# A top-32 attention kernel: the doubt test of each score tile moves from VectorE to GpSimd, and ranked values are kept for three tiles

## The reference

```python
scores = jnp.einsum('bhqd,bhkd->bhqk', q, kk) * scale
vals, idx = jax.lax.top_k(scores, k)          # k = 32 of 3136
w = jax.nn.softmax(vals, axis=-1)
vg = jnp.take_along_axis(v[:, :, None, :, :], idx[..., None], axis=3)
out = jnp.einsum('bhqk,bhqkd->bhqd', w, vg)
```

## Time and profile before

| | us |
|---|---|
| median of 3 runs | 34495.23 |
| the profiled execution | 34476.98 |
| its span in the trace | 34475.4 |
| VectorE busy | 28043.8 |
| TensorE matmuls busy | 26639.3 |
| ScalarE busy | 23766.6 |
| GpSimd busy | 19614.1 |

### The profile page before, as it was taken

The page is one execution under the profiler, slowest core; times in us unless marked ns, Lnnn a source line. Parts: engine busy times, 40 slices in busy tenths (PEclk is TensorE's granted clock), DMA queues, the critical chain, the costliest instruction groups (busy, mean ns, idle before and its releaser), DMA issues. The chain is left out here.

```text
span 34475.4 us, 624959 instructions
## 1 busy us (share of the span) xinstructions
PE 26639.3 (77%) x190808; PEld 11994.5 (35%) x190809; DVE 28043.8 (81%) x155761; ACT 23766.6 (69%) x29153; POOL 19614.1 (57%) x7792
## 2 busy tenths in 40 slices
PE   4656887788888888887258887888887788872589
PEld 4543333333333333333123333333333333331122
DVE  5557999899999999997769998999998999986421
ACT  1116887788888889886158897988887788871111
POOL 0005776677777777775037776777776677760000
PEclk7778998899999999998579998999998899985555
DMA  1001000000000000000110000000000000001100
GB/s 40 8 21 45 6 6 5 5 6 6 6 6 5 6 6 6 6 5 25 43 54 6 6 6 5 6 6 5 5 5 5 5 6 6 6 13 50 52 11 8
DMA packets 133222, 455.07 MB, mean 13 GB/s; under 512 B 29244, under 2 KB 85444, under 8 KB 111240
## 3 DMA queue, kind: packets, MB, share of 16 engines
q1 hardware_dynamic: 129256, 410.72, 3.6%
HBM read 244.71 MB, written 165.93 MB: 12 GB/s over the span
## 5 line engine op out<-in xcount | busy, mean ns | idle before, releaser
L232 POOL TENSOR_SCALAR Z<-S,M 128x3136 uint8<-128x3136 f32 (+1 forms) x2240 | 18383.3, 8212 | 6122.5 <-PE banks L336 5801.1
L510 DVE MAX8 C<-S 128x8 f32<-128x98 f32 x102400 | 19731.9, 252 | 1892.4 <-ACT S L421 1747.0
L421 ACT COPY S<-banks 128x896 f32<-128x896 f32 (+1 forms) x12800 | 10277.1, 821 | 1898.6 <-DVE C L510 676.8
L451 ACT ACTIVATE W<-banks 128x1024 f32<-128x1024 f32 (+1 forms) x9524 | 9801.9, 1030 | 1718.1 <-PE banks L336 1652.1
L327 PE MATMUL banks<-Q,K 99*128 99x512 bf16 (+2 forms) x22550 | 6434.5, 370 | 2666.4 <-ACT S L421 1410.1
L289 PE MATMUL banks<-K,Q 96*128 96x448 bf16 x22400 | 6566.7, 371 | 1422.6 <-ACT W L451 554.8
L372 PE MATMUL banks<-W,V 128*32 128x512 f32 (+1 forms) x45100 | 6843.3, 587 | 109.0 <-ACT W L454 78.9
L336 PE MATMUL banks<-NEG,Z 128*128 128x128 bf16 (+1 forms) x56300 | 6022.8, 224 | 0.0
L336 PEld LDWEIGHTS banks<-NEG,Z 128*128 128x128 fp8e4 x56300 | 4587.2, 101 | 1761.4 <-issue 255.9
L336 PE MATMUL banks<-NEG,ZA 128*128 128x128 bf16 (+1 forms) x24150 | 4779.2, 223 | 0.0
L327 PEld LDWEIGHTS banks<-Q,K 99*128 99x128 bf16 (+1 forms) x22550 | 1639.0, 99 | 7460.5 <-ACT S L421 3616.4
(11 more groups left out here) (204 smaller groups left out, 20819.6 us busy)
## 6 DMA issues: line engine op xcount, KB each, us to landing
q<-ln_o SPq DMA_DIRECT2D x20, 1568.0 KB, 5.1
ln_x<-y SPq DMA_DIRECT2D x16, 1568.0 KB, 6.0
K<-k_parts SPq DMA_DIRECT2D x130, 147.0 KB
Q<-q_parts SPq DMA_DIRECT2D x130, 147.0 KB
q_parts<-pj_parts SPq DMA_DIRECT2D x24, 784.0 KB, 4.7
k_parts<-pj_parts SPq DMA_DIRECT2D x24, 784.0 KB, 7.8
V<-v_rows SPq DMA_DIRECT2D x130, 112.5 KB, 7.4
v_rows<-pj_vt SPq DMA_DIRECT2D x8, 1800.0 KB, 11.8
```

The lines of the kernel that those rows point to most:

```text
L232: pool.tensor_scalar(mask_at(tile)[0:rows, :].bitcast(U8), m.S[0:rows, slot(tile), :], m.M8[0:rows, side(i), t, 31:32], None, ALU.is_lt).t ...
L421: act.copy(m.S[0:rows, slot(tile), at:at + CW * w].rearrange("p (a n) -> p a n", a=w), m.AB[0:rows, pair(score_at[a]):pair(score_at[a]) + ...
L451: ins = act.activation(m.W[:, e % 4, 0:n_banks, :], m.AB[:, b:b + n_banks, :], ACT.Exp)
L510: ins = dve.max(m.C[0:rows, tile % 2, TOP_AT + k:RANKED:CHUNKS], m.S[0:rows, slot(tile), CHUNK * k:CHUNK * k + CHUNK])
```

## The change

`doubt` becomes a function of GpSimd, called for every tile ahead of that tile's shifts and mask. VectorE no longer issues it. C keeps three tiles instead of two (RANKS = 3), and the first maximum of a tile waits until the test three tiles back has read its C. The flag matmul on TensorE still waits for `viol`, which GpSimd raises now.

```diff
+RANKS = 3
...
+            def doubt(tile):
+                i, t = divmod(tile, NT)
+                rows = tile_rows(t)
+                C = m.C[0:rows, tile % RANKS, :]
+                pool.wait_ge(found, tile + 1)
+                pool.tensor_scalar(m.VI[0:rows, t:t + 1], m.C8[0:rows, t:t + 1], C[:, 7:8],
+                                   m.M8[0:rows, side(i), t, 31:32], ALU.max, ALU.is_gt).then_inc(viol, 1)
...
             for i in range(n):
                 for t in range(NT):
+                    doubt(NT * i + t)
                     if t % 4 == 3 or t == NT - 1:
                         shift_parts(i, t // 4)
                     if maker(NT * i + t) == "P":
...
             def part_top(tile, k, checked=False):
                 rows = tile_rows(tile % NT)
+                if k == 0 and tile >= RANKS:
+                    dve.wait_ge(viol, tile - RANKS + 1)
...
-                ins = dve.max(m.C[0:rows, tile % 2, TOP_AT + k:RANKED:CHUNKS],
+                ins = dve.max(m.C[0:rows, tile % RANKS, TOP_AT + k:RANKED:CHUNKS],
...
-                C = m.C[0:rows, tile % 2, :]
+                C = m.C[0:rows, tile % RANKS, :]
...
-                def doubt():
-                    dve.wait_ge(found, tile + 1)
-                    dve.tensor_scalar(m.VI[0:rows, t:t + 1], m.C8[0:rows, t:t + 1], C[:, 7:8],
-                                      m.M8[0:rows, side(i), t, 31:32], ALU.max, ALU.is_gt).then_inc(viol, 1)
...
-                return steps + [final, doubt] + ([mask] if maker(tile) == "D" else [])
+                return steps + [final] + ([mask] if maker(tile) == "D" else [])
...
-            ("C", [128, 2, RANKED], F32), ("C8", [128, NT], F32), ("M8", [128, 2, NT, 32], F32),
+            ("C", [128, RANKS, RANKED], F32), ("C8", [128, NT], F32), ("M8", [128, 2, NT, 32], F32),
```

## The result

The change makes the kernel slower: a median of 35252.74 us over four runs, against 34495.45 for the kernel before. The ratio is 1.0222, with a 95% interval of 1.0204 to 1.024. That is +757 us where +864 was forecast, and 97 us under the 35,350 us named.

A forecast was written before the change was run, and what follows sets the result against it. The prediction took the ring of TensorE and ScalarE as the bound. 608 + 250 + 45 - 39 = +864 us on 34476.98 gave 35341, plus 18 for the median 35,359, rounded to 35,350 us; range 34,750 to 35,900.

The forecast's parts named there:

- the ring of TensorE and ScalarE: In the Heads stage, these two engines handing each other three pairs of banks set the pace; VectorE follows closely.
- Rival A: VectorE is the bound, so each 0.17 us saved per test counts: 544 us faster, 33,950 us; chance 0.04.
- Term 1, the stalls: TensorE's flag matmuls wait for tests queued behind GpSimd's masks, at five flags per head pair: 608 us slower.
- The 0.6 us of cover on ScalarE: At each stalled flag, ScalarE's later take-up of scores hides 0.6 us of TensorE's stall, 3.0 us per pair.
- if neighbouring waits hid 2 us each: Lower case for the flag stalls: waits nearby hide 2 us of each, leaving a loss near 250 us.
- Term 2, the clock: After TensorE stalls over 2 us its clock drops to 1.2 GHz: 1.3 us at three flags per pair, 250 us.
- Term 3, VectorE: At an even head's tile 3, VectorE's wait for GpSimd delays ScalarE's free score slot 0.7 us, 64 times: 45 us.
- The 7 us of waiting at tile 11: In the even head, VectorE waits some 7 us at tile 11 for GpSimd's test three tiles back.
- rival D: VectorE's 7 us wait at tile 11 holds up score slots in full: +320 us, 35,670, up to 36,000; chance 0.10.
- The gain, 39 us: For about five tiles after each of 46 searches, VectorE is the laggard and the removed tests save 39 us.
- rival B: The waits at the flags are hidden: from 71 us faster to 60 slower, 34,420 to 34,560; chance 0.10.
- C: Rival: ScalarE and TensorE regain most between two stalls: +70 to +300 us, 34,570 to 34,800; chance 0.08.

The follow-up runs named there:

- e5: Kernel before, every tile tested against the row's highest value, so no tile is in doubt and the 46 searches are left out: 33200.5 us, ratio 0.9629.
- e6: Kernel before with no test at all, hence no searches; the flags wait for `found` instead: 33207.7 us, ratio 0.9632.
- e2_ranks4: The change with ranked values kept for four tiles instead of three: 35238.99 us, ratio 1.021.
- e7_warm: The change with small matmuls that nothing reads ahead of four of the five stalling flag waits of a head pair: 35093.96 us, ratio 1.0186.
- e3_both: The change with each check group's last test back on VectorE and ranked values kept for four tiles: 34440.96 us, ratio 0.9977; run again 34451.37 us, 0.9979.
- e1_split: The change with the test of each check group's last tile back on VectorE, 19 of 25 staying on GpSimd: 34540.92 us, ratio 1.0008.

## Why the prediction was right

**The bound.** The forecast took the ring of TensorE and ScalarE for the pace, against VectorE's 81%. e5 and e6 show it (7 us between with and without the test), and e2_ranks4 shows it from the other side (2,080 us of VectorE's waiting exchanged for another kind, 14 to 41 us of time). Rival A is refuted: the busiest engine gave up 619.5 us and the kernel got slower, and without the test altogether it gained nothing.

**Term 1, the stalls: 608 us, right.** The five flags named are the five that stall, by 2.61, 1.61, 2.22, 4.04 and 2.32 us in the pair shown, where 2.7, 1.6, 1.9, 4.1 and 2.1 were worked out. Over the span it is 861 us, 359 times, against about 800, some 320 times. The surplus is not spread evenly. The flag of an even head's tile 24 stalls 188 us in all, 3.0 each where it stalls, where 1.94 x 64 = 124 was forecast; the even head's tile 7 gives 145, 27 less than forecast; and two flags that were to find their test in time, those of an odd head's tiles 11 and 15, wait 49 times for 21 us together. The test takes 0.376 us on GpSimd where 0.28 was taken (the bound was 0.5), too little to explain this.

What the stalls and the clock cost together was forecast as 858 us. Taking the six tests away gave 712 us (35252.74 - 34540.92) or, by the ratios, 738 with three ranked tiles, and 798 with four. The clock's part of them is estimated below as 120 to 145, which leaves 570 to 680 us for the stalls; 608 lies inside. The 0.6 us of cover on ScalarE was 0.4 in the row shown. One sum is wrong and went into nothing: if neighbouring waits hid 2 us each, 64 pairs would leave 190 us at most, not 250.

**Term 2, the clock: 250 us, right in kind and too large.** The low level behind the stall is in the rows (0.93 and 1.94 us). Of the 256 flags at the four places with the longer stalls, 192 have a low-clock stretch that begins within 1.5 us of them. The forecast counted three places, 3 x 64 = 192. That the two numbers agree is luck: the fourth place, the even head's tile 24, stalls longer than was worked out. What was left out is that other low-clock stretches disappear when these come: the change adds 103 in sum, not 192. The price of 1.3 us each fits e7_warm (1.15 to 1.4). At 103 stretches the clock's part of the loss is then rather 120 to 145 us, an estimate from these counts, which is enough to explain why the sum came out 107 us too high. The failing was in the count, not in the price.

**Term 3, VectorE: 45 us.** The slot wait of the even head's tile 3 was to grow by 0.7 us. It grew from 1.0 to 1.6 us in the pair shown, but in 48 places and not in 64, so the term should have been 34. The 7 us of waiting at tile 11 came as 3.43, 1.60 and 2.71 us at tiles 9 to 11. VectorE's room elsewhere held: ScalarE's wait for VectorE did not grow in sum (659.3 us), so rival D is refuted. With the stalls left in, all of VectorE's waiting is worth 14 to 41 us (e2_ranks4). When they are gone it is worth 100 (e3_both against e1_split), and this the forecast did not say.

**The gain, 39 us.** e3_both gains 67 and 74 us in its two runs from 19 of the 25 tests, nearly what rival B gave as the ceiling (71 us, or 63 with 48 places). Of the 51 us by which ScalarE's waits for VectorE fell, 27.8 are in the short slot waits and 23.5 in the waits of over 3 us, which come with the searches (e5, without them, has none over 1.0). e5 and e6 suggest that the second kind counts, since without searches shorter slot waits gave nothing. How much of the gain each kind gives stays open.

**Rivals B and C.** They needed the waits at the flags to be hidden. In the profile after they stand open, and the idle time of ScalarE grew with them.

## What to carry to other kernels

Before a small instruction is moved to an engine with room, look at what is ahead of it in that engine's queue and at who waits for its semaphore. Here tests of 0.38 us each cost 757 us in all, because they stood behind 8.2 us masks and an in-order TensorE waited for them. It was enough to keep the last test ahead of each flag, the one TensorE would wait for, on the quick engine (e1_split); the rest could move. And the busiest engine was not the bound here: it was the one that waited.

## What had not been expected of the hardware

That the clock falls after a short stall was forecast. That filling the stall pays was not: matmuls whose result nobody reads, 441.3 us of them, made a kernel 124 to 159 us faster although its flags came no sooner. The mean granted clock rose from 0.847 to 0.859 in the profiled runs.

The 128x1 test takes 0.376 us on GpSimd, more than the 0.23 us of the 128x1 operation with one input and more than the 0.26 us it took on VectorE, where only 0.17 us of it counted.
